# Attention over pairs of batches: one exponential for two batches, query and key transposes as the last of a turn

## The reference

```python
D, H = 256, 16
q = _to_heads(plin(xm, w_q, b_q))
k = _to_heads(plin(xm, w_k, b_k))
v = _to_heads(plin(xm, w_v, b_v))
qt, kt, vt = (logmap0(q), logmap0(k), logmap0(v))
scores = jnp.einsum('bhqd,bhkd->bhqk', qt, kt) / math.sqrt(HD)
attn = jax.nn.softmax(scores, axis=-1)
out_h = expmap0(jnp.einsum('bhqk,bhkd->bhqd', attn, vt))
attn_out = plin(_from_heads(out_h), w_o, b_o)
attn_t = g_msa * logmap0(attn_out)
x = mobius_add(residual, expmap0(attn_t))
```

## Time and profile before

| | |
|---|---|
| median of three runs | 1287.87 us |
| the profiled execution | 1287.52 us, span 1285.7 us |
| TensorE busy | 1096.9 us, 85% of the span |
| VectorE busy | 1040.2 us, 81% |
| ScalarE busy | 853.4 us, 66% |
| GpSimd busy | 605.3 us, 47% |
| the attention loop's full turns | about 490 to 935 us of the span |

### The profile page before, as it was taken

How to read it: one execution, slowest core, us unless ns; L and a number is a source line. 1 busy time by engine, 2 the same in 40 slices (tenths; PEclk the granted TensorE clock), 3 DMA queues, 4 the chain that set the end, 5 groups by cost and what they waited for, 6 DMA issues and landing times.

```text
span 1285.7 us, 20138 instructions
## 1 busy us (share of the span) xinstructions
PE 1096.9 (85%) x5760; PEld 783.9 (61%) x5782; DVE 1040.2 (81%) x2502; ACT 853.4 (66%) x2310; POOL 605.3 (47%) x1059
## 2 busy tenths in 40 slices
PE   8999967875895499999999999999988688888885
PEld 7888833332442287777777777777776345555554
DVE  6887758887787467888888888888987789989984
ACT  3545467877884246666666666666666788888873
POOL 2345236663575524334433444433421356667764
PEclk9999979997997799999999999999998889989998
DMA  7334221424976333334333433334225346666633
GB/s 246 105 112 103 97 81 45 176 111 144 375 232 187 98 99 82 99 99 98 86 88 91 99 88 89 87 99 99 60 61 127 67 97 164 164 164 165 164 99 115
DMA packets 116287, 156.32 MB, mean 122 GB/s; under 512 B 9296, under 2 KB 99536, under 8 KB 114640
## 3 DMA queue, kind: packets, MB, share of 16 engines
q1 hardware_dynamic: 115632, 155.03, 43.8%
q10 hardware_dynamic: 544, 0.00, 0.0%
HBM read 111.22 MB, written 27.00 MB: 108 GB/s over the span
## 4 chain that ended last, share of the span: by engine, by line
issue 24%; POOL 16%; PE 12%; DVE 9%; ACT 7%; POOLq 0%; DVEq 0%; ACTq 0%
POOL t_qk L1972 5%; POOL t_u L1902 4%; PE t_bk L1395 3%; POOL t_u L1907 3%; PE t_fB L1416 2%; PE t_bk L2034 1%; PE t_fA L2048 1%; ACT t_vbd L1460 1%; DVE t_qt L1628 1%; ACT t_vbd L1476 1%; ACT t_junk L1434 1%; PE t_bk L2022 1%; DVE t_bmax L1635 1%; PE t_fA L1378 1%; ACT t_y L1523 1%
## 5 line engine op out<-in xcount | busy, mean ns | idle before, releaser
L2034 PEld LDWEIGHTS t_bk<-t_vbd,t_pt 128*128 128x128 f32 x1024 | 133.4, 194 | 30.5 <-issue 19.3
L2034 PE MATMUL t_bk<-t_vbd,t_pt 128*128 128x66 f32 x1024 | 131.4, 273 | 18.5 <-ACT t_pt L2152 13.9
L2022 PE MATMUL t_bk<-t_qbd,t_kpar 128*128 128x256 f32 x512 | 135.9, 388 | 0.5 <-DMA t_qbd<-t_qt 0.5
L1395 PE MATMUL t_bk<-k_w12g,t_ut 128*128 128x512 f32 x256 | 126.5, 618 | 2.4 <-ACT t_ut L1516 1.2
L2022 PEld LDWEIGHTS t_bk<-t_qbd,t_kpar 128*128 128x128 f32 x512 | 92.8, 192 | 10.7 <-DMA t_qbd<-t_qt 0.9
L411 POOL TENSOR_SCALAR s_hleak<-s_hring,k_leak 128x128 f32<-128x128 f32 x128 | 47.6, 372 | 100.6 <-ACT s_hring L366 93.6
L2146 ACT ACTIVATE t_ysq<-t_y 128x768 f32<-128x768 f32 x64 | 53.8, 841 | 60.0 <-DVE t_y L2325 60.0
L2048 PE MATMUL t_fA<-k_wqkv,t_ut 128*128 128x512 f32 (+1 forms) x256 | 91.2, 500 | 1.2 <-ACT t_ut L2129 1.2
L1913 POOL TENSOR_SCALAR t_s_su<-t_s_ru 128x4 f32<-128x4 f32 x16 | 3.8, 236 | 180.8 <-ACT t_s_ru L2137 180.8
L2048 PE MATMUL t_fB<-k_wqkv,t_ut 128*128 128x512 f32 (+1 forms) x256 | 88.6, 489 | 0.0
L2152 ACT ACTIVATE t_pt<-t_bk 128x512 f32<-128x512 f32 x128 | 73.7, 587 | 21.7 <-PE t_bk L2022 20.2
(11 more groups left out here) (377 smaller groups left out, 3069.6 us busy)
## 6 DMA issues: line engine op xcount, KB each, us to landing
t_scb<-g_rows SPq DMA_DIRECT2D x64, 256.0 KB, 4.6
t_shb<-g_rows SPq DMA_DIRECT2D x64, 256.0 KB, 5.5
hidden_rows<-k_own SPq DMA_DIRECT2D x6, 1536.0 KB, 5.8
s_xrow<-in_x_dram SPq DMA_DIRECT2D x16, 512.0 KB, 3.6
k_hs<-s_hring SPq DMA_DIRECT2D x16, 512.0 KB, 3.1
b_xin<-in_x_dram SPq DMA_DIRECT2D x16, 512.0 KB, 4.4
x_rows<-b_xout SPq DMA_DIRECT2D x16, 512.0 KB, 5.1
t_xf<-x_rows SPq DMA_DIRECT2D x16, 512.0 KB, 4.7
```

What stands on the lines that cost most here:

```text
L1395: last = nc.tensor.matmul(z.fW[:, j, :], z.ut[:, c, j * P:(j + 1) * P], k["w12g"][:, c, :], start=False, stop=(c == C - 1))
L2022: last = nc.tensor.matmul(bk[e % 2][:, c * 4 * T:(c + 1) * 4 * T], kpar[:, c, e, :, :].rearrange("p a t -> p (a t)"), qbd[:, c, :, e * T:( ...
L2034: last = nc.tensor.matmul(bk[2 + e % 2][:, p * VW:(p + 2) * VW], pt[:, e % 2, p * T:(p + 2) * T], vbd[:, j, h, p:p + 2, :].rearrange("p c ...
```

## The change

`EPAIRS = GB // 2`: four pairs of batches. `exponentials(n)` takes banks 0 and 1 in one instruction of 1024 columns and writes one of two buffers of 1024 columns: `ptile`, which has the size of the old pt, and qt, which is otherwise free between the DMAs to qbd and the next copies. `scores(n)` makes the scores of both batches of a pair and waits for the exponential of the pair before, since both banks are in use together. score_ready and exp_ready count pairs.

TensorE's order in a full turn becomes products(0), scores(0), products(1), values(0) and (1), products(2), scores(1), products(3), scores(2), values(2) and (3), scores(3), values(4) and (5), values(6) and (7), turn_x, the o transposes, then the sixteen transposes of queries and keys, tile by tile, with a wait for each tile of qk, and wo. ScalarE's exponentials stand at e = 0, 2, 3 and 5, each ahead of the square of y_e, and ut comes ahead of ot.

```diff
-                    if e >= 2:
-                        pe.wait_ge(s["exp_ready"], (i - 1) * GB + (e - 1))
-                    for c in range(C):
-                        last = nc.tensor.matmul(bk[e % 2][:, c * 4 * T:(c + 1) * 4 * T], kpar[:, c, e, :, :].rearrange("p a t -> p (a t)"),
-                                                qbd[:, c, :, e * T:(e + 1) * T], start=True, stop=True)
+                    else:
+                        pe.wait_ge(s["exp_ready"], (i - 1) * EPAIRS + n)
+                    for e in (2 * n, 2 * n + 1):
+                        for c in range(C):
+                            last = nc.tensor.matmul(bk[e % 2][:, c * 4 * T:(c + 1) * 4 * T], kpar[:, c, e, :, :].rearrange("p a t -> p (a t)"),
+                                                    qbd[:, c, :, e * T:(e + 1) * T], start=True, stop=True)
                     last.then_inc(s["score_ready"], 1)
...
-                    pe.wait_ge(s["exp_ready"], (i - 1) * GB + (e + 1))
+                    pe.wait_ge(s["exp_ready"], (i - 1) * EPAIRS + (e // 2 + 1))
...
-                for e in range(GB + 1):
-                    if i == NG and e == 7:
-                        once(second.turn_u, 0)
-                    if mid and e < GB:
-                        scores(e)
-                    if mid and e >= 1:
-                        values(e - 1)
-                    if front and e < GT - 1:
-                        products(e + 1)
+                if mid:
+                    scores(0)
                 if front:
-                    pe.wait_ge(s["qk_ready"], (i + 1) * GT)
-                    if mid:
-                        pe.wait_ge(s["exp_ready"], i * GB)
-                    for b in range(C):
-                        turn_qk(b)
+                    products(1)
+                if mid:
+                    values(0)
+                    values(1)
+                if front:
+                    products(2)
+                if mid:
+                    scores(1)
+                if front:
+                    products(3)
+                if mid:
+                    for n in range(2, EPAIRS):
+                        scores(n)
+                        values(2 * n - 2)
+                        values(2 * n - 1)
+                if i == NG:
+                    once(second.turn_u, 0)
+                if mid:
+                    values(GB - 2)
+                    values(GB - 1)
                 if head:
                     turn_x(i + 1)
...
                 if front:
-                    for b in range(C, 2 * C):
-                        turn_qk(b)
+                    if mid:
+                        pe.wait_ge(s["exp_ready"], i * EPAIRS)
+                    for half in range(2):
+                        for j in range(GT):
+                            if half == 0:
+                                pe.wait_ge(s["qk_ready"], i * GT + j + 1)
+                            for b in (2 * half, 2 * half + 1):
+                                last = nc.tensor.transpose(bk[b][:, j * P:(j + 1) * P], qk[:, j, b * P:(b + 1) * P], k["ident"][:, :])
+                                if j == GT - 1:
+                                    last.then_inc(s["qkt_ready"], 1)
...
-                def exponentials(e):
-                    act.wait_ge(s["score_ready"], (i - 1) * GB + (e + 1))
-                    if e >= 2:
-                        act.wait_ge(s["pv_ready"], (i - 1) * GB + (e - 1))
-                    nc.scalar.activation(pt[:, e % 2, :], bk[e % 2][:, :], ACT.Exp, scale=1.0 / math.sqrt(HD)).then_inc(s["exp_ready"], 1)
+                def exponentials(n):
+                    act.wait_ge(s["score_ready"], (i - 1) * EPAIRS + (n + 1))
+                    if n >= 2:
+                        act.wait_ge(s["pv_ready"], (i - 1) * GB + 2 * (n - 1))
+                    nc.scalar.activation(pt[n % 2], bank[:, 0:2, :].rearrange("p r n -> p (r n)"), ACT.Exp, scale=1.0 / math.sqrt(HD)).then_inc(s["exp_ready"], 1)
...
-                    if mid:
-                        exponentials(e)
+                    if mid and e in (0, 2, 3, 5):
+                        exponentials((0, 2, 3, 5).index(e))
...
+                if head:
+                    turned_u(i + 1)
+                if i == NG:
+                    once(second.turned_u, 0)
                 if mid:
                     for cc in range(C):
                         act.wait_ge(s["otp_ready"], (i - 1) * C + (cc + 1))
```

More of the change, by code:

```diff
@@ L49 @@
 NBLK = D // BLK
+EPAIRS = GB // 2
 QMAX = 127.0
@@ L1358, in products @@
         elif self.t:
-            pool.wait_ge(self.t["score_ready"], NG * GB)
+            pool.wait_ge(self.t["score_ready"], NG * EPAIRS)
         pool.tensor_tensor(self.blocks(z.xd), self.blocks(z.q0), self.spread(z.bmax), ALU.mult).then_inc(s["xd_ready"], 1)
@@ L1385, in wide @@
         if g == 0 and self.t:
-            pe.wait_ge(self.t["exp_ready"], NG * GB)
+            pe.wait_ge(self.t["exp_ready"], NG * EPAIRS)
             pe.wait_ge(self.t["o_ready"], 2 * NG * GB)
@@ L1530, in turned_xd @@
         elif self.t:
-            act.wait_ge(self.t["score_ready"], NG * GB)
+            act.wait_ge(self.t["score_ready"], NG * EPAIRS)
         for c in range(C):
@@ L1652, in result @@
                 elif self.t:
-                    dve.wait_ge(self.t["score_ready"], NG * GB)
+                    dve.wait_ge(self.t["score_ready"], NG * EPAIRS)
             nc.vector.tensor_tensor(z.res[:, 2 * h:2 * h + 2, :], z.fM[:, h * 512:(h + 1) * 512].rearrange("p (j d) -> p j d", j=2),
@@ L1703, in attention_mlp @@
         vbd = m.sb("vbd", [P, GT, 2, PAIRS, VW])
-        pt = m.sb("pt", [P, 2, 2 * D])
+        ptile = m.sb("pt", [P, 4 * D])
         rden = m.sb("rden", [P, 2, PAIRS // 2, 2])
@@ L1751, in attention_mlp @@
         flat_qt = qt[:, :, :].rearrange("p c r -> p (c r)")
+        pt = (ptile[:, :], flat_qt)
         flat_qbd = qbd[:, :, :, :].rearrange("p c q r -> p (c q r)")
@@ L1865, in _ @@
                         sp.dma_start(qbd[r, :, p, :], qt[r, :, :]).then_inc(s["qbd_loaded"], 16)
-            sp.wait_ge(s["score_ready"], NG * GB)
+            sp.wait_ge(s["score_ready"], NG * EPAIRS)
             sp.dma_start(z.xin, row_group(k["x_dram"], 0)).then_inc(zs["xin_loaded"], 16)
@@ L2031, in values @@
                         pe.wait_ge(s["o_ready"], 2 * ((i - 1) * GB + e - 1))
-                    pe.wait_ge(s["exp_ready"], (i - 1) * GB + (e + 1))
+                    pe.wait_ge(s["exp_ready"], (i - 1) * EPAIRS + (e // 2 + 1))
                     for p in range(0, PAIRS, 2):
-                        last = nc.tensor.matmul(bk[2 + e % 2][:, p * VW:(p + 2) * VW], pt[:, e % 2, p * T:(p + 2) * T],
+                        at = e % 2 * PAIRS * T + p * T
+                        last = nc.tensor.matmul(bk[2 + e % 2][:, p * VW:(p + 2) * VW], pt[e // 2 % 2][:, at:at + 2 * T],
                                                 vbd[:, j, h, p:p + 2, :].rearrange("p c w -> p (c w)"), start=True, stop=True)
@@ L2224, in turn @@
                                              fB[:, cc * GR:(cc + 1) * GR].rearrange("p (e c t) -> p e c t", c=C, t=T), ACT.Copy).then_inc(s["ot_ready"], 1)
-                if head:
-                    turned_u(i + 1)
-                if i == NG:
-                    once(second.turned_u, 0)
                 if front:
```

8 lines of the change are left out of this document (2 added, 6 removed).

## The result

The changed kernel takes 1312.75 us (median of four runs, 1306.52 to 1314.46), the kernel before, run beside it on the same chip, 1288.17 us (1287.47 to 1290.62). The ratio is 1.0181, with a 95% interval of 1.0157 to 1.0204: 24.6 us slower, where 1320 us, 32 us slower, had been forecast. The profiled execution took 1312.94 us, its span is 1311.1 us, 25.4 more than the 1285.7 of before.

What follows compares the result with a forecast made beforehand. No engine was taken as full; a loop of waits bound the turn. Thirteen turns at +2.48 (1.1 loop, 1.4 clock) gave 32.2, ends -2.6 + 3.0 + 0: 1287.9 + 32.6 = 1320 us, range 1285 to 1333.

Steps and rivals of the forecast that it cites:

- The loop: Chain of one attention turn from `output(7)` back to `output(7)`: 23.44 + 11.68 = 35.1 against 34.02, +1.1 a turn.
- the square: ScalarE's square of y3: 1 us off the path before, now behind exponential 2 on the path, taking 0.87.
- The clock: TensorE's gap of 2.95 before `output(7)` ends lowers its clock; a low stretch costs 1.7, taken as 1.4 a turn.
- The ends: Turns outside the 13 full ones: turns 0 and 1 -2.6, turn 15 +3, turn 16 0.
- The sum: Whole kernel: 13 x 2.48 = 32.2, with -2.6 + 3.0 + 0 for the ends, +32.6 on 1287.9.
- (a): Rival: the attention loop lengthens as forecast, 1.1 a turn, but the clock stays full: 1303 us, chance 0.22.
- (b): Rival: the later scores stay hidden and the old loop holds: 1285 to 1289 us, chance 0.10.
- the old loop with the new tail: Turn if exponential 2 came early enough, its tail longer by 0.3: 34.2, so 33.9 to 34.2.
- (c): Rival: `output(7)` isn't the gate, TensorE's 32.16 a turn becomes the bound: down to 1261, half 1274, chance 0.14.
- (d): Rival: the low clock lasts through most of each turn, +3.5 to +5 a turn: 1335 to 1350 us, chance 0.06.

Runs made afterwards that it cites:

- y1: Changed kernel with the square of y3 ahead of the third merged exponential on ScalarE: 1309.08 us, ratio 1.0178.
- y2: Changed kernel with the square of y3 ahead of the third exponential and the last head norms ahead of `output(2)`: 1299.27 us, ratio 1.0086.
- v1: Changed kernel with eight query/key transposes back ahead of the x transposes and outputs 6 and 7 ahead of `moved()`: 1299.32 us over eleven runs.
- x2: Changed kernel with 2.6 us of matmuls, results unused, in TensorE's gap ahead of the second o transposes: 1300.08 us, ratio 1.0105.
- x4: Kernel before with only the transposes of queries and keys moved behind the o transposes: 1292.64 us, ratio 1.003.
- x3: Changed kernel with outputs 6 and 7 ahead of `moved()` on VectorE: 1258.94 us, ratio 0.9775.
- w1: Kernel before with the transposes of queries and keys last and outputs 6 and 7 ahead of `moved()`: 1264.06 us, ratio 0.9798.
- y4: Kernel before with outputs 6 and 7 ahead of `moved()` on VectorE: 1279.81 us, ratio 0.9942.
- x1: Changed kernel with the first eight transposes of queries and keys back ahead of turn_x: 1306.21 us, ratio 1.0161.
- z1: Changed kernel with outputs 6 and 7 ahead of `moved()`, square of y3 ahead of the third exponential, last head norms ahead of `output(2)`: 1253.22 us, ratio 0.9721.

## Why the prediction came out as it did

**The loop.** The step that decided was to follow the chain through the third exponential, the square, `moved()` and `output(7)`, and to sum it: 35.1 forecast, 34.85 measured. Part by part, between the rows of the two timelines shown:

| | forecast | measured |
|---|---|---|
| o transposes (half), 16 transposes | 2.20 | 2.24 (838.63 to 840.87) |
| wo | 3.54 | 3.46 |
| four products | 10.56 | 10.36 |
| six scores, values 0 and 1 | 6.88 | 6.9 |
| `output(7)` to the end of the third pair | 23.44 | 23.2 |
| exponential, square | 1.85 | 1.79 (826.95 to 828.74) |
| norms, totals, logarithm | 2.27 | 2.28 (to 831.02) |
| factors, outputs 4 and 5 | 2.37 | 2.36 |
| `moved()` | 3.45 | 3.46 |
| outputs 6 and 7 | 1.74 | 1.74 |
| `output(7)` to y0 | 9.9 | 9.8 |

The excess over 34.02 was 1.1 and is 0.83. The quarter comes mostly from the products, all four taken from one row of 2.80; three of them are 2.74 long, and the next group starts 2.57 behind them.

**A wait that was missed.** The sum was right for a reason that was only half of it. The text says that the old turn had the square 1 us off the path and that the new one puts it on it. But `output(2)` ends at the same moment: it waits 0.69 for values(2), which the new order puts behind the third pair of scores, and it stands in front of the last head norms. y1 shows that the square alone is worth 0.05 a turn, y2 that both are worth 0.43; the norms alone were not tried. Whoever had acted on the prediction's story would have made y1 and won nothing.

**The clock.** The size of one event was right: a low stretch was to cost 1.7, and costs 1.69. How often it comes was a choice between bounds of 0 and 2.9, not worked out, and this is the term that was mis-sized: 1.4 a turn would be five events in six turns, and there are seven in thirteen, 0.89 a turn. Of the 7.2 us by which the sum is too high 6.6 stand here. The trace of before had one low and one full case for such gaps; that it then came in about half of the turns agrees with them, but two cases give no share. The gap itself was forecast at 2.95 and is 2.79. By the Trainium skill ("TensorE: Matmul & The Clock Gate", section "HAM oscillation — how this bites in real kernels") the clock would have stayed full; the row at 516.18 and the low stretch of v1 behind 1.30 us don't agree with it, and x2 shows that the gap was the cause.

**The ends.** Turns 0 and 1 were to win 2.6 and won 2.30, through the late transposes (x4: 2.76). Turn 15 was to lose 3.0, and all behind it nothing: its wo begins 31.75 us behind y0 where it began 27.99, 3.8 more, of which about 1 is the clock (its 16 transposes take 2.96 for 1.91); turn 16's is 4.8 later, so that turn lost 1.0; what follows gave back 0.7. Together 4.1 for 3.0.

**The sum.** Forecast: 14.0 for the loop, 18.2 for the clock, 0.4 for the ends, 32.6. Measured in the profiled execution: 10.8, 11.6, 1.8, and 1.2 from ahead of the loop, 25.4.

**The rivals.** (a), the loop at full clock, 1303, is what x2 made: 1300. (b) fell: the later scores do lengthen the loop, though x4 shows the old loop with the new tail at the 34.2 that (b) was priced with. (c), that `output(7)` isn't the gate, was wrong for this kernel and right as a price: x3 takes the gate away and lands at 1259, just below the 1261 given for it, with TensorE as the bound as (c) said (31.48 a turn, not 32.16; w1, without the order by pairs, has 31.64, so most of this difference is not from the pairs, and its cause is open). Its condition, `moved()` without qk beside it, costs 1.80 there; half of 3.45 was forecast. (d), a clock that stays low, is seen nowhere in the changed kernel; v1 comes nearest, with about 6 us of every second turn of 36.

## What to carry to other kernels

A reordering on one engine pays only if the last wait of the turn lies on it: here the late transposes removed a wait for GpSimd, and VectorE's `output(7)`, which stood 3.4 us behind work that nobody waits for, took its place. Before judging a new order, put what the bound engine waits for ahead of what nobody waits for; the same change is then worth 1.6% (x3's 1258.94 against y4's 1279.81) instead of minus 1.8%. And when two waits end within a tenth of a microsecond of each other, both have to go: taking one away measures as nothing.

## What was not expected of the hardware

The clock fell behind gaps much shorter than the 2.75 of the earlier trace rows: behind 1.67 in 8 of 13 turns (x1), behind 1.30 in 13 of 13 in the one trace of v1, which is of one of its three longest executions, there by turns for about 6 and 3.4 us. Behind 1.94 it fell in none of the 13 turns of x4's trace, the shortest of its ten executions, behind 2.66 in 3 (y2), behind 2.79 in 7 (after). So the length of the gap alone does not decide: behind it stand 32 transposes in x1 and v1, and 20 in x4, y2 and the changed kernel. With the gap gone the same transposes leave the clock full (x2, x3, z1). Why it is mostly every second turn in the changed kernel and each turn in v1's trace was not settled.

VectorE's four scalar_tensor_tensor of `moved()` on 128x256 take 3.43 us beside GpSimd's tensor_tensor on 128x512 and 1.80 nearly without it (x3; one alone up to 1.28 us in the trace of the changed kernel, where its median in x3 is 0.47), while the outputs, which VectorE does beside the same GpSimd work in x3, keep their 0.61. One activation over two banks, 1024 columns, took 1.02 us, and 0.92 to the next instruction, against 0.58 and 0.48 for 512.
